# The last expert's down products lag five chunks and close group by group, and the last pair's chain stands in another order

## The chip, the cores and the metric

The kernel runs on one core of one Trainium2 chip. The metric is the device time of one execution in microseconds (us), here the median over several executions. Lower is better.

## What is computed

A block with attention and a mixture of experts, on 16 sequences of 100 tokens with 256 features each:

```python
x = x + attention(layernorm(x), ctx, ctx)      # 16 heads of 16, rope, window of 65 keys
n = layernorm(x).reshape(1600, 256)
topk_p, topk_i = top_k(softmax(n @ router_w.T), 2)
topk_p = topk_p / topk_p.sum(-1)
for e in range(8):                             # gate, up: 1024 x 256; down: 256 x 1024
    mask   = (topk_i == e).any(-1)
    mean_w = (topk_p * (topk_i == e)).sum() / mask.sum()
    x[mask] += mean_w * ((silu(n @ gate[e].T) * (n @ up[e].T)) @ down[e].T)
```

The weight of an expert is one number, the mean over its tokens, so it is known only when the last token has been routed.

## The kernel before

Each engine has a program of its own, written out by hand with semaphores (`s_...`). Engines are named as in the profile: PE (matrix products), DVE and ACT (element-wise work), POOL (small arithmetic and the DMAs that scatter rows), SP (which issues most other DMAs). What an engine's program lists first, it does first; nothing reorders the work.

**Attention.** The 16 sequences are taken in 8 pairs. The loop over `i` and `n` (0 to 7) is a software pipeline: in step `n` of turn `i` an engine does a piece of pair `i`, pieces of pair `i - 1` (output projection, residual), and pieces of pair `i - 2` (normalisation for the router, router, ranks). Scores are made in 64 portions `N`, each of 4 heads of a sequence. `den_transpose` turns the softmax denominators, `attend` (DVE) multiplies them in, `o_project` (PE) projects, `residual` (DVE) adds and takes the statistics, `rows_center` writes the centred rows of the last pair, `x2_transpose` and `route_logits` (PE) lead to `choose` (DVE), which picks two experts. `ranks` counts the tokens of each expert ahead of a token, and POOL's `scatter` writes each row twice into the list of its expert in DRAM (`slots`). `weights_low(-1, 1, k)` splits a sixth `k` of the first expert's weights into a high and a low part (`w_hi`, `w_lo`). `warm` and `idle` are products whose results nobody reads.

**Between the stages.** The first tile of the first expert isn't waited for: `early_tile` transposes what is in the list before the last two pairs, and `late_rows` adds the last two pairs' rows by products with one-hot columns. `here_columns` and `hot_column` make these. `plan` holds how many tiles each expert has.

**Experts.** A tile is 448 rows of one expert, in 4 groups (`GRP`) of 112. In this data each expert has one tile. The 1024 hidden features are 8 chunks (`FC`) of 128. For each chunk `f`, `hidden` makes 12 products for gate and up, ACT applies silu, DVE multiplies, ACT and DVE split the result into `h_hi` and `h_lo`. Experts 0 to 6 make the down products transposed (`columns_down`) and turn them back in the next tile. The last expert makes them in rows (`project_down`), 3 products for each group and chunk: chunk `f - 3` stands behind `hidden(f)`, and the last three chunks follow at the end, first for groups 0 and 1, whose bank is `b_o`, then for groups 2 and 3, whose bank is `b_small`. ACT's `take_output` scales a group into `y_sb`, and POOL adds its 112 rows to the output with an indirect DMA (L1500), four such DMAs in turn.

## Time and profile before

| | us |
|---|---|
| time, median of 3 runs | 466.39 |
| lowest and highest of the 3 | 465.91, 467.24 |
| the profiled execution, its own time | 467.31 |
| its span, first to last instruction | 465.5 |
| PE busy in the span | 443.7 |
| ACT busy | 281.8 |
| DVE busy | 302.2 |
| POOL busy | 138.3 |

Times in the trace count from the start of the span. The profiled execution took 1.81 us more than its span. A matrix product's bar in the timeline is longer than the distance to the next one, since they are pipelined; the distance is what counts in a row of them. For a sequence of like products the timeline gives one row with a count.

### The profile page before, as it was taken

What the parts mean: (1) busy time and instruction counts of PE and PEld (TensorE: products, weight loads), DVE (VectorE), ACT (ScalarE), POOL (GpSimd) and SP (SyncE); (2) the same over time, 40 slices, a digit from 0 to 9 for tenths busy, and PEclk for the clock granted to TensorE, in tenths of its full rate; (3) what the DMA queues carried; (4) which work ended last, traced back from release to release, by engine and by line L of the source; (5) the groups of instructions that cost most, each with busy time, mean ns of one, the idle gap of its engine ahead of it and who ended that gap; (6) DMA issues with size and microseconds to landing.
All of it is one profiled execution on the core that took longest, in us unless ns stands there. A gap on an engine that the chain in (4) does not pass through costs nothing.

```text
span 465.5 us, 8569 instructions
## 1 busy us (share of the span) xinstructions
PE 443.7 (95%) x2553; PEld 358.7 (77%) x2553; DVE 302.2 (65%) x744; ACT 281.8 (61%) x886; POOL 138.3 (30%) x172
## 2 busy tenths in 40 slices
PE   7999999999999999999999999999999999999980
PEld 4657565657566655579999999999999999999980
DVE  3766969798989878787646647467474563763320
ACT  2388778888787888356456456465554655554230
POOL 5201014453626252575014040050220500403122
PEclk9899999999999999899999999999999999999995
DMA  5640092030303032416727636465375453311102
GB/s 166 222 110 8 18 336 73 13 103 18 106 14 112 8 110 68 128 55 199 253 86 180 212 69 180 142 144 172 93 202 174 92 175 85 42 40 21 21 10 30
DMA packets 24667, 49.90 MB, mean 107 GB/s; under 512 B 5730, under 2 KB 15494, under 8 KB 24474
## 3 DMA queue, kind: packets, MB, share of 16 engines
q1 hardware_dynamic: 12858, 22.95, 16.4%
q10 hardware_dynamic: 5616, 19.40, 14.2%
q0 software_dynamic: 6144, 6.97, 8.6%
q8 instruction: 21, 0.34, 0.3%
q14 instruction: 28, 0.23, 0.2%
HBM read 39.16 MB, written 13.20 MB: 112 GB/s over the span
## 4 chain that ended last, share of the span: by engine, by line
PE 80%; DVE 7%; ACT 5%; issue 3%; DMA 1%; POOL 1%; SPq 0%; ACTq 0%; POOLq 0%; DVEq 0%
PE b_s L767 8%; PE b_s L771 8%; PE b_s L768 8%; PE b_small L795 7%; PE b_o L795 7%; PE b_s L490 6%; PE b_pv L513 4%; ACT probs L942 3%; PE b_proj L543 3%; PE b_pt L499 3%; PE b_pt L767 3%; PE b_pt L771 3%; PE b_pt L768 3%; PE b_proj L569 3%; PE b_s L488 3%
## 5 line engine op out<-in xcount | busy, mean ns | idle before, releaser
L942 ACT ACTIVATE probs<-b_s,negmax 100x100 f32<-100x100 f32 x256 | 85.7, 361 | 19.4 <-DVE negmax L1278 19.2
L1500 POOL DMA_INDIRECT out<-y_sb,idnow x32 | 46.8, 1462 | 153.1 <-ACT y_sb L1002 129.8
L975 ACT CAST h_hi<-h_sb 128x448 fp32r<-128x448 f32 x64 | 36.3, 567 | 85.7 <-DVE h_sb L1362 85.7
L1254 DVE TENSOR_TENSOR w_lo<-w_raw,w_hi 128x1024 fp32r<-128x1024 f32 x48 | 58.8, 1224 | 19.5 <-ACT w_hi L906 19.5
L767 PE MATMUL b_s<-x_hi,w_lo 128*128 128x448 f32 x192 | 71.1, 370 | 0.0
L771 PE MATMUL b_s<-x_lo,w_hi 128*128 128x448 f32 x192 | 69.5, 362 | 0.0
L768 PE MATMUL b_s<-x_hi,w_hi 128*128 128x448 f32 x192 | 69.3, 361 | 0.0
L1366 DVE TENSOR_TENSOR h_lo<-h_sb,h_hi 128x448 fp32r<-128x448 f32 x64 | 40.1, 626 | 40.5 <-ACT h_hi L975 40.5
L942 ACT ACTIVATION_READ_ACCUMULATOR probs<-b_s,negmax 100x1 f32 x256 | 56.9, 222 | 0.0
L490 PE MATMUL b_s<-kblk,qrot 128*100 128x400 f32 x128 | 53.6, 499 | 0.0
L906 ACT CAST w_hi<-w_raw 128x1024 fp32r<-128x1024 f32 x48 | 50.4, 1050 | 0.0
L1278 DVE TENSOR_REDUCE negmax<-b_s 100x4 f32<-100x400 f32 x64 | 36.2, 565 | 20.1 <-PE b_s L490 19.8
L1362 DVE TENSOR_TENSOR h_sb<-b_s,act 128x448 f32<-128x448 f32 x32 | 19.8, 620 | 35.2 <-PE b_s L771 35.2
L971 ACT ACTIVATE act<-b_s 128x448 f32<-128x448 f32 x64 | 34.6, 540 | 11.5 <-PE b_s L771 11.3
L1455 POOL DMA_INDIRECT slots<-xrow,desti x32 | 35.3, 1103 | 14.0 <-issue 7.6
L771 PEld LDWEIGHTS b_s<-x_lo,w_hi 128*128 128x128 f32 x192 | 36.0, 188 | 2.7
L767 PEld LDWEIGHTS b_s<-x_hi,w_lo 128*128 128x128 f32 x192 | 36.1, 188 | 2.3 <-ACT x_hi L967 0.3
L499 PEld LDWEIGHTS b_pt<-cst,probs 100*100 100x100 f32 x256 | 26.1, 128 | 15.2 <-issue 14.3
L768 PEld LDWEIGHTS b_s<-x_hi,w_hi 128*128 128x128 f32 x192 | 36.0, 188 | 2.1
L922 ACT COPY probsT<-b_pt 100x400 f32<-100x400 f32 x64 | 32.2, 503 | 4.5 <-PE b_pt L499 4.2
L513 PE MATMUL b_pv<-probsT,v_sb 100*32 100x200 f32 x256 | 31.0, 344 | 3.1 <-ACT probsT L922 2.4
L499 PE MATMUL b_pt<-cst,probs 100*100 100x100 f32 x256 | 32.6, 249 | 0.3 <-ACT probsT L922 0.2
(201 smaller groups left out, 896.7 us busy)
## 6 DMA issues: line engine op xcount, KB each, us to landing
w_raw<-in_ffw ACTq DMA_DIRECT2D x36, 512.0 KB, 4.0
w_raw<-in_ffw SPq DMA_DIRECT2D x12, 512.0 KB, 5.5
slots<-in_padrows SPq DMA_DIRECT2D x9, 449.8 KB, 4.6
xin<-slots SPq DMA_DIRECT2D x9, 449.8 KB, 4.5
kblk<-krot SPq DMA_DIRECT2D x120, 12.5 KB, 1.8
out<-x_all SPq DMA_DIRECT2D x8, 200.0 KB
ctx_all<-in_ctxT SPq DMA_DIRECT2D x1, 1200.0 KB, 6.3
x_all<-in_x SPq DMA_DIRECT2D x1, 1200.0 KB
```

Source lines behind the costliest of these rows:

```text
L490: pe.matmul(o, qrot[:, i % 2, 2 * c + b, :], kblk[:, i % 2, c, h:h + QH, b * S:(b + 1) * S], start=False, stop=True).then_inc(s_s, 1)
L499: m = pe.transpose(b_pt[0:S, h * S:(h + 1) * S], probs[:, N % 3, h, :], ident[0:S, 0:S])
L513: m = pe.matmul(b_pv[32 * j:32 * j + 32, c * PT:(c + 1) * PT], v_sb[:, i % 2, b, c * P + 32 * j:c * P + 32 * j + 32], probsT[:, N % 3, 2 * ...
L767: pe.matmul(o, wl[:, c, cols], x_hi[:, c, :], start=(c == 0), stop=False)
L768: pe.matmul(o, wh[:, c, cols], x_hi[:, c, :], start=False, stop=False)
L771: m = pe.matmul(o, wh[:, c, cols], x_lo[:, c, :], start=False, stop=(c == DC - 1))
L795: m = pe.matmul(b_y[c][:, 0:TILE], left[:, f, c * P:(c + 1) * P], right[:, f, :], start=(f == 0 and k == 0), stop=(f == FC - 1 and k == 2))
L906: nc.scalar.copy(w_hi[1 - par][:, cols], w_raw[:, cols]).then_inc(s_whi, 1)
L942: m = nc.scalar.activation(probs[:, N % 3, h, :], b_s[N % 3][0:S, h * S:(h + 1) * S], ACT.Exp, bias=negmax[:, N % 4, h:h + 1], accum_out=p ...
L1254: V.tensor_tensor(w_lo[1 - par][:, cols], w_raw[:, cols], w_hi[1 - par][:, cols], ALU.subtract).then_inc(s_wlo, 1)
L1366: V.tensor_tensor(h_lo[:, f, :], h_sb[:, f % 2, :], h_hi[:, f, :], ALU.subtract).then_inc(s_hlo, 1)
L1500: G.indirect_dma_start(out, bass.IndirectOffsetOnAxis(idnow[:, n:n + 1], 0), y_sb[:, n, :], None, bounds_check=TOK + TILE - 1, oob_is_err= ...
```

## The change

Five things are done.

1. **The last expert's down products.** Chunk `f - 5` stands behind `hidden(f)` instead of `f - 3`, and the last five chunks follow at the end, group by group: all of group 0, then 1, 2 and 3. Groups 0 and 2 are in `b_o`, 1 and 3 in `b_small`. Each group has a signal of its own.
2. **The last pair's chain.** The residual, the statistics and the centring are done for each of the two sequences apart (`last_residual`), the first while the second is still in attention. `den_transpose` of the last sequence stands before two portions of values. `rows_low(NPAIR - 2)` and, for the last pair's turn, `rows_write` come later. The early tile and the one-hot products are split into pieces between other steps, and the counts of `warm` differ.
3. **The sixth chunk of the first expert's low weights** is made after `meanw`, not during the last pair; PE waits for five chunks at the start of the first expert, and for the sixth before chunk 4 of its down products. SP loads the next weights into that sixth accordingly later.
4. **The start.** SP sends x before the context; the constants go in two pieces, of which the second (4 x 376 bytes a partition of 4 x 1014) goes behind the other weights. The counts of `idle` are 10, 3 and 6 instead of 8, 2 and 3.
5. **The first tile's row numbers** (`idnext`, 448 numbers of 4 bytes) are fetched by a DMA from POOL's queue, behind the scatters, instead of from SP's.

```diff
@@ SP
-            load_rows(0, 0, 1)
-            sp.dma_start(cst[:, :], consts).then_inc(s_cst, 16)
+            sp.dma_start(x_all[:, 0:2, :], x[0:2].rearrange("b s d -> s b d")).then_inc(s_x[0], 16)
+            sp.dma_start(ctx_all[:, :, 0:PT], ctxT[:, :, 0:PT]).then_inc(s_ctx[0], 16)
+            sp.dma_start(cst[:, 0:C_TRI], consts[:, 0:C_TRI]).then_inc(s_cst, 16)
...
-            for k in range(NPAIR - 3, WCH):
-                second_weights(k)
...
+            for k in range(NPAIR - 3, WCH):
+                second_weights(k)
...
-            sp.dma_start(idnext[:, :].bitcast(F32),
@@ PE
                     if n == 5 and i == NPAIR:
-                        warm(5)
-                        early_tile()
-                        warm(5)
+                        warm(8)
                         x2_transpose(NPAIR - 1)
                     if n == 5 and 0 <= i - 2 < NPAIR:
                         ranks(i - 2)
-                    if n == 2 and prv:
+                    if n == 5 and i == NPAIR:
+                        early_tile(0)
+                    if n == 2 and prv and i < NPAIR:
                         den_transpose(2 * i - 1)
...
+                    if n == 1 and i == NPAIR:
+                        den_transpose(2 * i - 1)
...
-            warm(5)
+            late_rows(NPAIR - 2, (1,))
+            warm(2)
             late_rows(NPAIR - 1)
...
-                    o = b_y[g // 2][0:ROWS, g % 2 * D:(g % 2 + 1) * D]
+                    o = b_y[g % 2][0:ROWS, g // 2 * D:(g // 2 + 1) * D]
...
-                    if f == FC - 1 and g % 2:
+                    if f == FC - 1:
                         m.then_inc(s_down, 1)
...
-                    if f >= 3:
-                        (project_down if last else columns_down)(par, t, f - 3)
+                    if f >= 5 and last:
+                        project_down(par, t, f - 5)
+                    elif f >= 3 and not last:
+                        columns_down(e, par, t, f - 3)
...
+                for g in range(GRP):
+                    if g >= DC:
+                        pe.wait_ge(s_y, GRP * t + GRP + g - DC + 1)
+                    for f in range(FC - 5, FC):
+                        project_down(par, t, f, (g,))
                 tile_transpose(t + 1)
...
-                pe.wait_ge(s_wlo, WCH * (e + 1))
+                pe.wait_ge(s_wlo, WCH * (e + 1) if e else WCH - 1)
@@ ACT
                 for n in range(GRP):
-                    if n % 2 == 0:
-                        a.wait_ge(s_down, 2 * t + n // 2 + 1)
+                    a.wait_ge(s_down, GRP * t + n + 1)
@@ DVE
-            def rows_center(i):
...
+            def last_residual(b):
+                i = NPAIR - 1
+                v.wait_ge(s_o, 2 * i + b + 1)
+                v.wait_ge(s_xob, i + 1)
+                xs = x_all[:, 2 * i + b, :]
+                done = s_x2 if b else s_x2a
+                V.tensor_tensor(xs, b_o[0:S, b * D:(b + 1) * D], xs, ALU.add).then_inc(done, 1)
+                v.wait_ge(done, i + 1 if b else 1)
+                link(V.bn_stats(stats2[:, b, :], xs))
+                ins = V.bn_aggr(mv2[:, b, :], stats2[:, b, :])
...
+                V.tensor_scalar(xn[:, b, :], xs, mv2[:, b, 0:1], None, ALU.subtract).then_inc(s_xc, 1)
...
                     if n == 1 and i == NPAIR:
-                        rows_low(NPAIR - 2)
+                        last_residual(0)
...
-                        residual(i - 1)
-                        rows_center(i - 1)
+                        last_residual(1)
...
+                    if n == 3 and i == NPAIR:
+                        rows_low(NPAIR - 2)
...
+            weights_low(-1, 1, WCH - 1)
             for e in range(E - 1):
@@ POOL, behind the last scatter
+            for q in s_scat:
+                g.wait_ge(q, 16 * TOPK * 2 * (NPAIR // 2))
+            g.wait_ge(s_tails[0], 16)
+            G.dma_start(idnext[:, :].bitcast(F32),
```

How the rows of an engine's program stand shows the first two of these best. **PE, end of the last pair's attention**, before: behind the transposes of the last probabilities, from the values (`b_pv`) through the denominators (`rdenx`) and the router's logits (`xn2T`) to the output projection (`att`).

```order
L513 MATMUL b_pv<-probsT,v_sb 32x200 [waits s_pTc]
L513 MATMUL b_pv<-probsT,v_sb 32x200
L513 MATMUL b_pv<-probsT,v_sb 32x200 [waits s_pTc]
L513 MATMUL b_pv<-probsT,v_sb 32x200
L577 MATMUL b_small<-cst,rdenx 128x100 [waits s_x2Tc,s_rx]
L577 MATMUL b_small<-cst,rdenx 128x100
L647 MATMUL b_s<-mask_bf,ident_bf 100x400 x2
L612 MATMUL b_small<-rw_sb,xn2T 100x8 [waits s_rTc,s_x2Tc]
L612 MATMUL b_small<-rw_sb,xn2T 100x8 x3
L647 MATMUL b_s<-mask_bf,ident_bf 100x400
L589 MATMUL b_o<-attw,att 100x256 [waits s_att]
```

The same place in the changed program:

```order
L583 MATMUL b_small<-cst,rdenx 128x100 [waits s_x2Tc,s_rx]
L583 MATMUL b_small<-cst,rdenx 128x100
L519 MATMUL b_pv<-probsT,v_sb 32x200 [waits s_pTc]
L519 MATMUL b_pv<-probsT,v_sb 32x200
L519 MATMUL b_pv<-probsT,v_sb 32x200 [waits s_pTc]
L519 MATMUL b_pv<-probsT,v_sb 32x200
L620 MATMUL b_small<-rw_sb,xn2T 100x8 [waits s_rTc,s_x2Tc]
L620 MATMUL b_small<-rw_sb,xn2T 100x8 x3
L655 MATMUL b_s<-mask_bf,ident_bf 100x400 x4
L597 MATMUL b_o<-attw,att 100x256 [waits s_x2a,s_att]
```

The two transposes of the denominators now stand ahead of the values, and four unread products (`mask_bf`) stand in one piece before the projection.

**DVE, the same stretch**, before: behind the last denominators (`rdenx`), up to the centred rows (`xn`), without the seven rows of `choose` in the middle, which are the same in both programs.

```order
L1126 COPY rdenx<-rden 100x256 [waits s_rT,dve]
L1254 TENSOR_TENSOR w_lo<-w_raw,w_hi 128x1024 [waits s_whi]
L1219 TENSOR_TENSOR xr_lo<-xrow,xr_hi 100x512 [waits s_xrh]
L1133 SCALAR_TENSOR_TENSOR ev<-b_pv,cst,rdenT 128x200 [waits s_rTc,s_pv]
L1135 SCALAR_TENSOR_TENSOR ev<-b_pv,cst,rdenT 128x200
L1140 TENSOR_TENSOR att<-ev 128x200 [waits s_o,dve]
```

```order
L1185 TENSOR_TENSOR sel<-cst,choice 100x32
L1146 TENSOR_TENSOR x_all<-b_o,x_all 100x512 [waits s_xob,s_o,dve]
L1062 BN_STATS stats<-x_all 100x6 [waits s_x2]
L1062 BN_STATS stats<-x_all 100x6
L1066 BN_AGGR mv<-stats 100x2 [waits dve]
L1066 BN_AGGR mv<-stats 100x2
L1154 TENSOR_SCALAR xn<-x_all,mv 100x256 [waits s_var2]
L1154 TENSOR_SCALAR xn<-x_all,mv 100x256
```

And changed:

```order
L1138 COPY rdenx<-rden 100x256 [waits s_rT,dve]
L1169 TENSOR_TENSOR x_all<-b_o,x_all 100x256 [waits s_xob,s_o]
L1171 BN_STATS stats<-x_all 100x6 [waits s_x2a]
L1172 BN_AGGR mv<-stats 100x2 [waits dve]
L1178 TENSOR_SCALAR xn<-x_all,mv 100x256 [waits dve]
L1145 SCALAR_TENSOR_TENSOR ev<-b_pv,cst,rdenT 128x200 [waits s_rTc,s_pv]
L1147 SCALAR_TENSOR_TENSOR ev<-b_pv,cst,rdenT 128x200
L1152 TENSOR_TENSOR att<-ev 128x200 [waits s_o,dve]
```

```order
L1208 TENSOR_TENSOR sel<-cst,choice 100x32
L1169 TENSOR_TENSOR x_all<-b_o,x_all 100x256 [waits s_xob,s_o,dve]
L1171 BN_STATS stats<-x_all 100x6 [waits s_x2]
L1172 BN_AGGR mv<-stats 100x2 [waits dve]
L1178 TENSOR_SCALAR xn<-x_all,mv 100x256 [waits s_var2]
```

The split of weights (`w_lo`) and of rows (`xr_lo`) left this stretch, half of the residual work came ahead of `ev`, and only half of it is left behind `sel`. `xr_lo` now stands behind the four rows of counts and differences that follow `xn`, ahead of the writing of the last pair's rows (`xrow`).

**ACT, the last expert's output**, before:

```order
L988 ACTIVATE y_sb<-b_o,meanw 112x256 [waits s_down]
L988 ACTIVATE y_sb<-b_o,meanw 112x256
L987 REGISTER_ALU
L988 ACTIVATE y_sb<-b_small,meanw 112x256 [waits s_down]
L988 ACTIVATE y_sb<-b_small,meanw 112x256
```

And changed:

```order
L999 ACTIVATE y_sb<-b_o,meanw 112x256 [waits s_down]
L998 REGISTER_ALU
L999 ACTIVATE y_sb<-b_small,meanw 112x256 [waits s_down]
L998 REGISTER_ALU
L999 ACTIVATE y_sb<-b_o,meanw 112x256 [waits s_down]
L998 REGISTER_ALU
L999 ACTIVATE y_sb<-b_small,meanw 112x256 [waits s_down]
```

ACT waited for PE twice, for two groups each; now it waits four times, for one group each.

## Rows read from the trace of the kernel before

**Rows 1.** The page: span, and TensorE's clock in 40 slices, in tenths.

```profile
span 465.5 us, 8569 instructions
...
PEclk9899999999999999899999999999999999999995
```

**Rows 2.** Stretches: us; busy PE, PEld, DVE, ACT, POOL; clock, DMA share, GB/s.

```profile
12.00:13.00 1.00, 1.00 (x5) 1.00 (x4) 0.91 (x3) 0.00 (x0) 0.00 (x0) 0.52 0.93 250
194.00:196.00 2.00, 2.00 (x7) 1.25 (x6) 1.02 (x5) 0.00 (x0) 0.00 (x0) 0.50 0.67 220
250.00:440.00 190.00, 190.00 (x1012) 178.26 (x1011) 108.64 (x154) 102.13 (x170) 37.21 (x31) 1.00 0.47 120
```

**Rows 3.** Timeline of the start: start us, us, engine, line, operation.

```profile
5.90 1.62 PE L543 MATMUL b_proj<-ctx_all,attw 128*128 128x200 f32 x8
7.19 0.75 DVE L1062 BATCH_NORM_STATS2 stats<-x_all 100x6 f32<-100x256 f32 x2 [4.99 <-DMA x_all<-in_x]
...
7.36 1.52 PE L675 MATMUL b_s<-blank 128*128 128x400 bf16 x8
...
10.36 0.53 PE L526 MATMUL b_small<-cst,xn 100*128 100x100 f32 x4 [1.49 <-DVE xn L1078]
...
11.53 2.52 PE L543 MATMUL b_proj<-xnT,attw 128*128 128x200 f32 x8 [0.29 <-issue]
```

**Rows 4.** Timeline from the last pair's attention to the first expert.

```profile
190.11 1.18 PE L513 MATMUL b_pv<-probsT,v_sb 100*32 100x200 f32 x8
...
191.26 0.69 DVE L1219 TENSOR_TENSOR xr_lo<-xrow,xr_hi 100x512 fp32r<-100x512 f32 x1 [0.39 <-ACT xr_hi L901]
...
192.08 0.43 DVE L1133 SCALAR_TENSOR_TENSOR ev<-b_pv,cst,rdenT 128x200 f32<-128x200 f32 x1
...
193.29 2.03 PE L589 MATMUL b_o<-attw,att 128*100 128x256 f32 x4
...
194.32 0.18 DVE L1185 TENSOR_TENSOR sel<-cst,choice 100x32 f32<-100x32 f32 x1
...
195.42 0.69 DVE L1146 TENSOR_TENSOR x_all<-b_o,x_all 100x512 f32<-100x512 f32 x1 [0.92 <-DVE sel L1185]
...
197.21 0.62 DVE L1154 TENSOR_SCALAR xn<-x_all,mv 100x256 f32<-100x256 f32 x2
...
203.65 0.44 PE L666 MATMUL b_proj<-onehot,xr_hi 100*128 100x448 f32 x1
...
206.51 0.47 PE L767 MATMUL b_s<-x_hi,w_lo 128*128 128x448 f32 x1
```

**Rows 5.** Scatters by line (ns min/median/max), then timeline of the second tile's inputs.

```profile
L1455 POOL DMA_INDIRECT slots<-xrow,desti x32: 984/993/1751, 74.7 to 215.1; - x32
...
214.78 1.23 DVE L1254 TENSOR_TENSOR w_lo<-w_raw,w_hi 128x1024 fp32r<-128x1024 f32 x1 [0.30 <-ACT w_hi L906]
...
219.88 0.64 SPq L443 DMA_DIRECT2D idnext<-slots  x1
223.49 0.38 SPq L434 DMA_DIRECT2D xin<-slots  x1
...
229.11 0.56 PE L754 MATMUL b_proj<-cst,xin 112*128 112x112 f32 x4
...
231.10 0.16 DVE L1356 COPY idnext<-xin 112x4 int32<-112x4 int32 x1
```

**Rows 6.** Chain of work at the end; then two rows of the timeline.

```profile
445.86 0.70 PE b_o L782 x6
...
449.36 2.14 PE b_small L782 x18
...
456.15 1.45 POOL out L1500
...
447.15 0.62 DVE L1366 TENSOR_TENSOR h_lo<-h_sb,h_hi 128x448 fp32r<-128x448 f32 x1 [0.63 <-ACT h_hi L975]
...
450.85 1.47 POOL L1500 DMA_INDIRECT out<-y_sb,idnow  x1 [16.03 <-ACT y_sb L988]
```

More of the change, by code:

```diff
@@ L52 @@
 assert MAXTILES < 1 << FIELD
-C_ID, C_TRI, C_ONE, C_MASK = 0, 128, 256, 384
-C_ROPE = C_MASK + S
-C_PAR = C_ROPE + 4 * S
-C_EXP = C_PAR + 2
+C_ID, C_ROPE = 0, 128
+C_MASK = C_ROPE + 4 * S
+C_HEAD = C_MASK + S
+C_PAR = C_HEAD + HC
+C_TRI = C_PAR + 2
+C_ONE = C_TRI + 128
+C_EXP = C_ONE + 128
 C_BASE = C_EXP + E
@@ L593, in x2_transpose @@
             def x2_transpose(i):
-                if i == NPAIR - 1:
-                    pe.wait_ge(s_xc, 1)
-                else:
+                if i < NPAIR - 1:
                     pe.wait_ge(s_xr, i + 1)
@@ L661, in late_rows @@
                 k = i - NPAIR + 2
-                for b in range(2):
+                for b in halves:
                     pe.wait_ge(s_hotA if b else s_hot, k + 1)
@@ L720, in _ @@
                         if i < 0:
-                            idle(8)
+                            idle(10)
                         xn_transpose(i + 1)
@@ L726, in _ @@
                         values(N - 3)
-                    if n == 2 and i == NPAIR:
-                        warm(2)
                     if n == 2 and 0 <= i - 2 < NPAIR:
@@ L807, in output_transpose, with block @@
                         m.then_inc(s_yt, 1)
-            def block(t, par, last, lo):
+            def block(t, e, par, last, lo):
                 for f in range(FC):
@@ L925, in _ @@
                         top_exponentials(i - 2)
-                    if n == 1 and i == NPAIR:
+                    if n == 2 and i == NPAIR:
                         rows_high(NPAIR - 2)
@@ L1149, in residual @@
                 norm_stats(xs, stats2, mv2, s_var2)
-            def rows_center(i):
-                v.wait_ge(s_var2, i + 1)
-                for b in range(2):
-                    ins = V.tensor_scalar(xn[:, b, :], x_all[:, 2 * i + b, :], mv2[:, b, 0:1], None, ALU.subtract)
-                ins.then_inc(s_xc, 1)
+            def last_residual(b):
[8 more added lines that the diff above has]
+                ins = V.bn_aggr(mv2[:, b, :], stats2[:, b, :])
+                if b:
+                    ins.then_inc(s_var2, 1)
+                    v.wait_ge(s_var2, i + 1)
+                else:
+                    link(ins)
+                V.tensor_scalar(xn[:, b, :], xs, mv2[:, b, 0:1], None, ALU.subtract).then_inc(s_xc, 1)
             def rows_write(i):
@@ L1325, in _ @@
                         attend(2 * i)
-                    if n == 6 and prv:
+                    if n == (7 if i == NPAIR - 1 else 6) and prv:
                         rows_write(i - 1)
```

80 lines of the change are left out of this document (43 added, 37 removed).

## The prediction

> **What bounds the kernel now.** I read the page first, then the busy time by stretches, then the chain of work and the timeline at three places. The span is 465.5 us [rows 1]. From 250 to 440 us PE is busy for 190.00 of 190 us at the full clock [rows 2]. The experts, from 206.51 us [rows 4] to the last down product, which ends at 449.36 + 2.14 = 451.50 us [rows 6], are a solid block of products. The change neither adds nor removes a product that counts there, so a gain can only come from the three ends of such blocks: the start, the stretch between attention and the first expert, and what follows the last product. In each the reader should look for what is waited for last.
>
> At the end, POOL's four output DMAs stand one behind the other: the first starts at 450.85, the last at 456.15, and the span ends 465.5 - 456.15 = 9.35 us after that [rows 1, 6]. That remainder (the last DMA's own time, its landing, the closing) I take as fixed.
>
> In the clock row two slices show an 8 [rows 1], the second of them at the last pair. In 12 to 13 us the clock was 0.52 and in 194 to 196 us it was 0.50, that is 1.2 instead of 2.4 GHz, though PE was busy in both [rows 2]. Before the first fall PE stood still from 7.36 + 1.52 = 8.88 to 10.36 us [rows 3].
>
> **The end, term one.** A chunk of down products is 12 products. 18 of them took 2.14 us, 0.117 to 0.119 each, so a chunk is 1.41 us (0.70 + 0.71) and a group's five chunks (15 products) are 1.76 us. Before, hidden(7) was over at 445.86, when chunk 4 began [rows 6]. With a lag of five, two chunks fewer stand ahead of it: it is over at 445.86 - 2.81 = 443.05. Then come chunk 2 (to 444.46) and the groups, to 446.21, 447.97, 449.73 and 451.50. PE ends when it ended before. Before, the first half was closed at 449.36 and POOL's DMA began at 450.85, 1.49 later, with ACT's copy in between [rows 6]; applied to group 0, its DMA begins at 446.21 + 1.49 = 447.70. POOL's own step is (456.15 - 450.85) / 3 = 1.77 us, the same as PE's step of a group, so both rules put the fourth at 452.99 or 453.00 in place of 456.15. **Term: -3.16 us.** A new wait could be group 0's last chunk on `h_lo(7)`. It was there at 447.15 + 0.62 = 447.77, 1.91 us after hidden(7) [rows 6], so it is there by 444.96; PE asks for it after four chunks at 444.46 + 1.41 = 445.87. Group 2 asks for group 0 to be copied out: that is so before POOL starts at 447.70, and it begins at 447.97. Bounds: 0 if POOL found something else to wait for, and at most -3.3, since its four steps can't shrink.
>
> **The start, term two.** x landed at 7.19, second in its queue, and the first context chunk before 5.90, first in it [rows 3]. They are 200 KB each, so I expect them to swap: x near 5.9, the context near 7.2. The key projection, at 5.90 before, then starts 1.3 us later, takes 7.36 - 5.90 = 1.46 us until the next product, and the ten idle products behind it (1.52 us for eight, 1.9 for ten) last until some 10.4. The transposes of xn began at 10.36 [rows 3]. So the earlier x gains nothing by itself; PE is behind it. What is gained is the clock: PE now stands still hardly at all before 11.5, and the query projection, 2.52 us at the low clock against 1.62 for eight like products at the high one [rows 3], is shorter by 0.9. **Term: -0.9 us.** Bounds: +0.1 (the clock falls anyway, and the queue of idle products is a little longer), and -2.2 (the context lands as early as before too, and all of the 1.3 us counts besides). I take the middle, since both ends need something that the rows speak against. Scores, keys and values behind it follow from this projection.
>
> **Between the stages, term three.** By its own clock, before any shift:
> - The attention product `ev` began at 192.08, though the values ended at 190.11 + 1.18 = 191.29; it waited for the denominators, whose transposes stood behind the values [rows 4]. Turned round, it can start at 191.4. I take 191.6, because `rows_write(6)` moved behind the last maximum delays PE's transposes of these rows by an estimated 0.2 us. That is -0.5.
> - `choose` then ends by 194.32 + 0.18 - 0.45 = 194.05. The output projection, 193.29 before, starts at 192.8 and takes 2.03 us at the low clock or about 1.0 at the high one [rows 4]: done at 193.8 or 194.8. The residual, 195.42 before, starts at 194.1 (high clock).
> - From there to the end of centring were 197.21 + 0.62 - 195.42 = 2.41 us for two sequences [rows 4]. For one I take 1.5, more than half since the handovers remain: done at 195.6 in place of 197.83, -2.2. The first sequence's half runs before 191.6, where the split of weights (1.23 us by its kind [rows 5]) and of rows (0.69) stood.
> - That 0.69 [rows 4] returns behind the centring, ahead of the last rows' writing: -1.55 remains, and all of DVE's chain up to the last one-hot columns carries it.
> - PE, between the counts and the last rows' products, has four products of 0.2 and two unread ones instead of five unread ones, and gets to the former 203.65 some 0.2 us later than DVE allows. **Term: -1.35 us**, the first expert at 205.16 instead of 206.51 [rows 4]. Bounds: -0.6 if the clock is low again at the projection (residual at 194.8), and -2.2 if the 0.69 and the 0.2 find room.
>
> **Edits costed at nothing.** The sixth split (1.23 us) now lies ahead of DVE's first work for the expert, which waits for PE's products anyway; PE asks for it six chunks later. It now stands beside POOL's eight scatters. One of these took 1.751 us against a median of 0.993, and it began at 215.1, just behind the start of a split at 214.78 [rows 5]; so I allow them 0.8 us. The Trainium skill, "SBUF — State Buffer", SBUF: two separate sides, says that a VectorE operation with two SBUF inputs and a GpSimd operation that reads SBUF lock each other out for a whole instruction; the slow scatter agrees with this, and by that rule this edit speaks against the change.
> What the scatters delay is the second tile. SP fetched it at 223.49, 3.6 us after it could send `idnext` at 219.88, and PE turned it at 229.11 [rows 5]. Now the scatters start 1.35 to 1.6 us earlier, SP has one DMA less ahead of it (0.64), and PE comes 1.35 earlier: the slack grows by 0.6 to 0.9, which pays the 0.8. If the cover were gone, each us late would be a us of the total.
> `idnext` itself has no row on POOL. Its nearest rows are 0.64 us for the issue on SP [rows 5] and 1.45 us for POOL's 112 rows of output [rows 6], which for 448 elements would be 5.8. From 218.3 with 5.8 and a landing of some 4 it is there by 228; DVE asks for it at 231.10 - 1.35 = 229.75 [rows 5]. Nothing, by either end. The Trainium skill, "DMA: Bandwidth & Descriptors", Issuing engine by pattern, gives simple loads to Sync and calls that path the faster one; by the first-byte figures of its Specifications the move costs 0.4 us, which would be hidden as well.
>
> **Sum.** -3.16 - 0.9 - 1.35 = -5.4 us. The profiled execution, 467.31, becomes 461.9. It stood 0.92 above the median of 466.39, from which the sum gives 461.0. I predict 461.4.
>
> **Rivals.**
> - *The clock falls again in the last pair* (0.2). Its stretch still holds few wide products, and the lengths of its pauses are new. Against it: four unread products in one piece, and more behind. If it falls at the projection, 0.75 is given back; if earlier, over values and logits too, up to 1.7: 462.2 to 463.1.
> - *The start gives nothing* (0.12), because the clock falls there as before: 462.3.
> - *The start gives the whole 1.3 as well* (0.08), as the context is early: 460.1.
> - *The last expert's end gives only half* (0.03): ACT or POOL answer single groups later, or the DMAs land more slowly: 463.0.
> - *The change doesn't do what it says* (0.03): POOL's first DMA starts hardly sooner, and the start gives nothing: 461.4 + 3.2 + 0.9 = 465.5, within 0.3%.
> - *Slower* (0.02). POOL's `idnext` comes so late that DVE stands before the last chunk of the first tile. My upper end leaves 229.75 - 228 = 1.75 us; beyond that each us counts, and from 1.75 + 5.4 = 7.2 us beyond my upper end it decides the sign. At 9 us it gives 461.4 + 7.2 = 468.6.
> The forecast keeps 0.52; its own range is 460.3 to 462.4.
>
> **The numbers.** About 0.3% (1.4 us) is what a measurement of this kernel can tell from no change. All cases but the last two lie beyond it: faster 0.95, same 0.03, slower 0.02. The range takes in the forecast, the clock and both cases of the start: 459.3 to 463.4.
>
> **What would show it.** After: POOL's last four DMAs begin 1.76 apart while PE still multiplies, the first some 3.8 us before PE's last product, the last 1.5 behind it. The clock is 1.00 from 12 to 15 us, the query projection under 1.7 us, while the key projection starts near 7.2. The output projection takes about 1.0 us, the first expert's first product comes near 204.3 in the span (206.51 less 2.25), and PE has no idle time at the second tile. I would be wrong if the clock row kept an 8 at the last pair, if PE waited before group 0's last chunk, or if POOL's DMAs were further apart than before.

## The result, and the profile after

| 13 executions each | before | after |
|---|---|---|
| median, us | 466.32 | 464.93 |
| lowest, highest | 465.91, 467.50 | 460.74, 465.64 |
| profiled execution, us | 467.31 | 465.43 |
| its span, mean clock | 465.5, 0.982 | 463.3, 0.984 |

The ratio of after to before is 0.9939 (95% interval 0.9919 to 0.9960): faster by 1.4 us in the medians, by 2.8 in the means (466.44 and 463.61), whose quotient the ratio is, and by 467.31 - 465.43 = 1.88 in the profiled executions. Predicted were 461.4 and at most 463.4.

The medians hide that the 13 times of after fall apart. The mean granted clock goes with them, but for 462.95: 460.74 and 460.85 at 0.993, 461.29 at 0.995, 461.43 at 0.994; then 462.26 and 462.95 (0.988, 0.984); and seven from 464.93 to 465.64, all at 0.983 or 0.984. The profiled execution is one of the last. Its page shows where the clock went: one slice of 40 at half, which answers to [rows 1].

```profile
span 463.3 us, 8586 instructions
...
PEclk9999999999999999959999999999999999999997
```

The stretches by busy time (us; busy PE, PEld, DVE, ACT, POOL; clock, DMA share, GB/s) answer to [rows 2]:

```profile
12.00:13.00 1.00, 1.00 (x8) 0.64 (x7) 0.62 (x3) 0.50 (x2) 0.00 (x0) 1.00 0.99 314
197.00:199.00 2.00, 1.22 (x7) 0.78 (x8) 1.83 (x13) 0.75 (x2) 1.14 (x4) 1.00 0.00 0
199.00:201.00 2.00, 2.00 (x11) 1.67 (x12) 1.82 (x9) 1.41 (x3) 1.23 (x3) 0.53 0.00 0
201.00:205.00 4.00, 4.00 (x14) 3.56 (x12) 1.47 (x9) 0.88 (x2) 2.75 (x5) 0.50 0.43 117
205.00:209.00 4.00, 4.00 (x14) 3.60 (x14) 3.00 (x11) 1.96 (x4) 3.27 (x3) 0.50 0.63 208
209.00:210.00 1.00, 1.00 (x6) 0.92 (x5) 0.00 (x0) 0.26 (x1) 0.70 (x2) 0.83 0.84 109
250.00:430.00 180.00, 180.00 (x948) 168.67 (x947) 105.22 (x148) 99.16 (x166) 35.76 (x30) 1.00 0.48 126
```

The fall at 12 us is gone. Before the experts the clock is low from 199.1 to 209.3 us, 10.2 us against 3.4 before (193.0 to 196.4), though PE is busy there without a break. My first theory came from the row ahead of it: in 197 to 199 PE was busy for 1.22 of 2 us.

The timeline of the start, beside [rows 3], is the first part below. The second, beside [rows 4], goes from the last pair's attention to the first expert. L597 is the output projection, L1169 the halved residual, L655 `warm`, L635 the ranks, L673 `late_rows`, L776 the experts' first product.

```profile
5.17 0.75 DVE L1073 BATCH_NORM_STATS2 stats<-x_all 100x6 f32<-100x256 f32 x2 [2.95 <-DMA x_all<-in_x]
...
6.62 1.59 PE L549 MATMUL b_proj<-ctx_all,attw 128*128 128x200 f32 x8 [0.94 <-DMA ctx_all<-in_ctxT]
...
9.74 0.51 PE L532 MATMUL b_small<-cst,xn 100*128 100x100 f32 x4
...
10.87 1.59 PE L549 MATMUL b_proj<-xnT,attw 128*128 128x200 f32 x8
...
15.85 0.50 PE L496 MATMUL b_s<-kblk,qrot 128*100 128x400 f32 x1
...
190.07 0.43 DVE L1145 SCALAR_TENSOR_TENSOR ev<-b_pv,cst,rdenT 128x200 f32<-128x200 f32 x1 [0.57 <-PE b_pv L519]
...
191.38 1.03 PE L597 MATMUL b_o<-attw,att 128*100 128x256 f32 x4
...
192.53 0.42 DVE L1169 TENSOR_TENSOR x_all<-b_o,x_all 100x256 f32<-100x256 f32 x1
...
193.60 0.87 PE L610 MATMUL b_small<-cst,xn 100*128 100x100 f32 x4
193.67 0.35 DVE L1178 TENSOR_SCALAR xn<-x_all,mv 100x256 f32<-100x256 f32 x1
...
196.90 0.44 PE L673 MATMUL b_proj<-onehot,xr_hi 100*128 100x448 f32 x1 [0.28 <-DVE onehot L1259]
...
197.78 0.33 PE L655 MATMUL b_s<-mask_bf,ident_bf 100*100 100x400 bf16 x1
...
198.89 0.21 PE L635 MATMUL b_small<-chosen,tri_bf 100*100 100x16 bf16 x1 [0.78 <-DVE chosen L1214]
...
199.13 0.72 PE L673 MATMUL b_proj<-onehot,xr_hi 100*128 100x448 f32 x1
...
201.17 0.84 PE L673 MATMUL b_proj<-onehot,xr_hi 100*128 100x448 f32 x1
...
205.97 0.84 PE L776 MATMUL b_s<-x_hi,w_lo 128*128 128x448 f32 x1
```

From `ev` to the last ranks the chain is earlier, and by more than the start's shift. The scores begin at 15.85 instead of 17.42 (-1.57). `ev` comes at 190.07 instead of 192.08: -2.01, of which -0.44 is its own. The centred rows end at 193.67 + 0.35 = 194.02 instead of 197.21 + 0.62 = 197.83: -3.81, own -2.24. The last pair's one-hot products begin at 201.17 instead of 203.65, and here the clock already eats: the products that follow the first are 0.37 us apart, not 0.20. The first expert begins at 205.97 against 206.51 [rows 4]; of 3.8 us gained 0.5 are left.

At the end (ACT's copy of a group and POOL's DMA, beside [rows 6]):

```profile
447.32 0.47 ACT L999 ACTIVATE y_sb<-b_o,meanw 112x256 f32<-112x256 f32 x1 [1.98 <-PE b_o L791]
...
452.56 0.47 ACT L999 ACTIVATE y_sb<-b_small,meanw 112x256 f32<-112x256 f32 x1 [1.29 <-PE b_small L791]
...
448.70 1.48 POOL L1531 DMA_INDIRECT out<-y_sb,idnow  x1 [12.67 <-ACT y_sb L999]
450.49 1.47 POOL L1531 DMA_INDIRECT out<-y_sb,idnow  x1 [0.30 <-issue]
...
454.03 1.47 POOL L1531 DMA_INDIRECT out<-y_sb,idnow  x1 [0.30 <-issue]
```

POOL's DMAs start 1.77 to 1.79 us apart, and the first goes while PE multiplies for group 1.

### The profile page after: what moved, and what is told of

Its sections match the earlier page's. It is cut to its first block, busy times and chain, and to the rows that moved or that the text cites. A ratio compares the mean times of both kernels' runs of the same rounds, so it can differ in the third digit from the quotient of the medians.

```text
span 463.3 us, 8586 instructions
## 1 busy us (share of the span) xinstructions
PE 444.0 (96%) x2551; PEld 360.9 (78%) x2551; DVE 302.8 (65%) x745; ACT 281.4 (61%) x886; POOL 138.6 (30%) x173
## 4 chain that ended last, share of the span: by engine, by line
PE 54%; POOL 1%; issue 1%; DVE 1%; ACT 0%; POOLq 0%
PE b_s L776 8%; PE b_s L780 8%; PE b_s L777 8%; PE b_small L806 7%; PE b_o L806 7%; PE b_pt L776 3%; PE b_pt L780 3%; PE b_pt L777 3%; POOL out L1531 1%; PE b_o L791 1%; PE b_pv L815 1%; PE b_proj L815 1%; PE b_proj L763 1%; PE b_pv L763 1%; PE b_proj L673 1%
## 5 line engine op out<-in xcount | busy, mean ns | idle before, releaser
L776 PE MATMUL b_s<-x_hi,w_lo 128*128 128x448 f32 x192 | 71.8, 374 | 0.0
L776 PEld LDWEIGHTS b_s<-x_hi,w_lo 128*128 128x128 f32 x192 | 36.6, 190 | 2.2
```

The lines of the kernel that those rows point to most:

```text
L776: pe.matmul(o, wl[:, c, cols], x_hi[:, c, :], start=(c == 0), stop=False)
```

## The experiments

Sixteen kernels ran, in four groups of four, each group on one chip and beside before. Before took 466.44 in the first group, but 472.93, 467.80 and 468.62 in the others, with a wider scatter, so a time is compared within its group. Only the second and the fourth group hold the changed kernel unaltered.

The last column counts executions with a mean clock of 0.988 or less, a line that I chose between the two kinds of the first table. It is a rough sign. The mean takes in every fall, wherever it stands, and the low clock behind PE's last products, 4.7 us in f2_changed_third's profile and 8.0 in f3_fill_again's, 0.005 to 0.009 of the mean; a fall of 3.4 us is worth 0.004. So short falls can hide above the line (a2_end's profile has one, at 0.989). The column is compared only between kernels with the new start.

| kernel | median, us (runs) | ratio to before, 95% | mean clock 0.988 or less |
|---|---|---|---|
| a1_fill | 461.27 (4) | 0.9890, 0.9875 to 0.9904 | 0 of 4 |
| a2_end | 463.56 (5) | 0.9934, 0.9921 to 0.9947 | 0 of 5 |
| a3_start | 465.82 (12) | 0.9986, 0.9978 to 0.9995 | 8 of 12 |
| a4_start_end | 462.78 (5) | 0.9922, 0.9909 to 0.9935 | 0 of 5 |
| b1_changed_again | 463.74 (4) | 0.9804, 0.9745 to 0.9862 | 2 of 4 |
| b2_fill_behind | 466.67 (6) | 0.9873, 0.9825 to 0.9921 | 2 of 6 |
| b3_before_pause | 472.18 (12) | 0.9994, 0.9961 to 1.0027 | 11 of 12 |
| b4_middle_fill | 465.84 (7) | 0.9859, 0.9816 to 0.9903 | 3 of 7 |
| e1_early_late | 463.15 (6) | 0.9886, 0.9835 to 0.9937 | 0 of 6 |
| d1_fill_three | 461.19 (6) | 0.9852, 0.9802 to 0.9901 | 0 of 6 |
| c1_fill_ids_sp | 461.58 (6) | 0.9862, 0.9814 to 0.9910 | 1 of 6 |
| c2_before_again | 470.11 (1) | | 1 of 1 |
| f1_narrow | 463.26 (6) | 0.9861, 0.9812 to 0.9910 | 3 of 6 |
| f2_changed_third | 462.13 (6) | 0.9872, 0.9825 to 0.9919 | 3 of 6 |
| f3_fill_again | 461.13 (6) | 0.9844, 0.9800 to 0.9888 | 1 of 6 |
| f4_wide_ahead | 461.70 (6) | 0.9860, 0.9809 to 0.9911 | 1 of 6 |

**a1_fill: the pause filled.**

```diff
                         late_rows(NPAIR - 2, (0,))
-                        warm(1)
+                        warm(5)
```

> The changed kernel with warm(5) in place of warm(1) behind the first half of the late rows: PE's pause of 0.78 us before the last pair's ranks, after which the granted clock fell to 0.50 at 199.2 us, is filled with four unread products of 0.2 us each. Theory (the clock that fell behind this pause is what is missing): the clock stays 1.00 from 199 to 210 us, the experts' first product comes near 203.2 in place of 205.97, every run lies between 460 and 462 and the median is 460.9. Rival 1 (the fall comes from the whole thin stretch, 184 to 199 us, or from outside the program, and not from this pause): nothing changes, the runs still fall into two groups, near 461 and near 465.4, median above 463. Rival 2 (the four products only delay the ranks and what follows): clock 1.00, but the first expert's product no earlier than 204, 462 or more.

Measured: 461.27, all four between 460.77 and 461.38. By stretches (columns as above), then the experts' first product:

```profile
197.00:199.00 2.00, 1.90 (x16) 1.29 (x15) 1.82 (x14) 0.54 (x1) 0.90 (x4) 1.00 0.00 0
199.00:201.00 2.00, 2.00 (x12) 1.78 (x12) 1.79 (x9) 1.42 (x3) 1.42 (x3) 1.00 0.00 0
201.00:205.00 4.00, 3.99 (x24) 3.34 (x23) 3.49 (x18) 3.00 (x5) 2.69 (x5) 1.00 0.42 117
```

```profile
202.86 0.47 PE L776 MATMUL b_s<-x_hi,w_lo 128*128 128x448 f32 x1
```

The clock is 1.00, and the first product comes 3.11 us earlier than after's 205.97. From the output projection (191.13) to the experts' first product it takes 11.73 us; in after's profile it took 14.59. The unaltered changed kernel was also caught once with the clock at 1.00 throughout (f2_changed_third, last part), and took 203.29 - 191.60 = 11.69. So the four products themselves neither cost nor bring anything; what was missing is the clock. That they kept it up in these four executions does not yet show that they always do, and the pause turns out not to be the cause, as told below.

**a2_end, a3_start, a4_start_end: the parts alone.** These are the kernel before with the hunks of the diff for the last expert's end, for the start (with the `idle` counts), and for both.

> The kernel before with the last expert's end alone (lag of five chunks, groups closed one by one, a signal for each). Theory: this term is 3.2 us wherever the block of experts stands: 466.3 - 3.2 = 463.1, POOL's last DMA 3.2 us sooner than before (near 453.0), PE's last product where it was (451.5), clock before the experts as before. Rival (a part of the end's 3.2 us in the changed kernel came from the later block or from the sixth chunk's place): 464.5 or more, with POOL's four DMAs more than 1.8 us apart or PE waiting for h_lo in the first group.

> The kernel before with the start alone (x first, constants in two pieces, idle products 10, 3 and 6). Theory: x lands near 5.2, the transposes of xn start at 9.7, the query projection takes 1.6 us at the full clock, the first scores come 1.56 us earlier, and nothing behind gives it back: 466.3 - 1.6 = 464.7. Rival 1 (the gain is given back at the last pair, since the pauses or the clock there shift): 465.5 to 466.5, with the clock low for longer than the 3.4 us of before. Rival 2 (the clock at the start and the later clock are one account: what PE does early is taken later): the mean clock of the execution stays at 0.982.

> Start and end together, the last pair and everything between the stages as before. Theory (the terms add up): 466.3 - 1.6 - 3.2 = 461.5, that is 3 us faster than the changed kernel's median, because the clock does not fall for 10 us; all runs within 1 us. Rival (an execution that runs ahead by 1.6 us meets the clock's fall by itself): two groups of runs, or a median above 463.

The end alone gave 466.44 - 463.56 = 2.9 in the medians (by the ratio 3.1, interval 2.5 to 3.7). The start alone gave 0.6, though its profile has the scores at 15.77, the first expert 1.53 earlier than in [rows 4] (204.98) and its own time 1.4 below before's profiled 467.31. Both together gave 3.7, close to 2.9 + 0.6; the theory's 461.5 was missed by 1.3, most of it at the start. From a4_start_end to a1_fill, which adds the rest of the change and the fill, it is 462.78 - 461.27 = 1.5. In a4_start_end the clock was 1.00 at the last pair, and PE stood still all the same:

```profile
191.64 1.11 PE L594 MATMUL b_o<-attw,att 128*100 128x256 f32 x4
...
195.08 0.60 PE L659 MATMUL b_proj<-cst,xin 112*128 112x112 f32 x4 [1.48 <-DMA xin<-slots]
...
196.75 0.42 PE L607 MATMUL b_small<-cst,xn 100*128 100x100 f32 x3
```

The early tile's rows (L659) landed at 195.08. The centred rows, ready at 195.30, were turned (L607) at 196.75, behind the tile and five unread products. In before's first profile the projection at the low clock took that time instead. So the old order lost it in either case, once to the clock and once to a DMA.

**c2_before_again** is before once more, for a second profile.

> The kernel before itself, for a second profile of it. In the first one, 467.31 us, the clock was low twice, 3.4 us each, at the start and in the last pair, with a mean of 0.982; most of its other executions show 0.988 to 0.991 and 466.4. Theory (a typical execution loses only one of the two stretches, and the one at the last pair costs nothing, because PE then waits for the early tile's DMA instead): the mean clock is near 0.99, one of the two stretches is missing, and if it is the one at the last pair, PE shows a wait of about 1.4 us for the early tile's rows. Rival: both stretches are there again, and 467.3 was high for another reason.

Half of it came: one low stretch of 3.4 us in place of two, the mean clock 0.986. But it was the one at the start that was missing: the query projection took 1.59 us, and the scores began at 16.71 where [rows 3]'s execution had them at 17.42. The one at the last pair was there (192.1 to 195.5). The time, 470.11, was high for a reason of another kind, told under the last heading.

**e1_early_late: the early tile moved, nothing else of the last pair's chain.** a4_start_end with `early_tile()` behind `x2_transpose` and `ranks`.

> Start and end as changed, the last pair as before, with one edit in it: the early tile's eight transposes stand behind the transposes of the last pair's centred rows and its ranks (and the five unread products in front of them and the five behind become ten in one piece). In the run with start and end alone PE stood still for 1.48 us until the early tile's DMA was there at 195.08, and turned the centred rows, ready at 195.30, only at 196.75. Theory (what the last pair's new order brings is this wait, more than the halved residual): the centred rows are turned at 195.4, the experts' first product comes near 203.3 instead of 204.62, and the time is 1.3 us below start and end alone: ratio to before 0.9895, where start and end alone had 0.9922. Rival (the chain on DVE decides, the wait was hidden): ratio 0.992, first product at 204.3 or later. If the clock falls in the thin stretch as in the changed kernel: runs 1.5 to 4.5 us above the lowest.

```profile
193.11 1.11 PE L594 MATMUL b_o<-attw,att 128*100 128x256 f32 x4
...
196.82 0.56 PE L607 MATMUL b_small<-cst,xn 100*128 100x100 f32 x4 [0.91 <-DVE xn L1160]
...
197.41 0.58 PE L659 MATMUL b_proj<-cst,xin 112*128 112x112 f32 x4
...
198.72 0.79 PE L617 MATMUL b_small<-rw_sb,xn2T 128*100 128x8 f32 x8
...
205.35 0.47 PE L772 MATMUL b_s<-x_hi,w_lo 128*128 128x448 f32 x1
```

From the projection to the turning it is 3.71 us instead of 5.11, as expected, but from the projection to the experts' first product 12.24 instead of 12.98: 0.74 and not 1.4. The tile's eight transposes, 0.8 us, now stand ahead of the logits (turning to logits 1.90 us). In a1_fill, where only half of them stand there, this distance is 11.73. The first product was expected near 203.3 and came at 205.35, since in this execution the projection itself was 1.47 us later than in a4_start_end (193.11 against 191.64). The median's interval is too wide to add to that.

**b4_middle_fill, c1_fill_ids_sp.** The first is before with the rest of the change and the filled pause, but start and end as before; the second is a1_fill with the row numbers sent from SP.

> The kernel before with the last pair's chain, the sixth chunk and the row numbers' DMA as changed, and with the pause before the ranks filled by four unread products; start and end as before. Theory (terms add up): the changed kernel with the filled pause had 461.3 and start with end alone 462.8, so this part is worth 1.5 us: 466.4 - 1.5 = 464.9. Rival 1 (it is worth more than that alone, 2.5 us or more, and part of it was lost beside the earlier start, where the DMA of the early tile lands last): 464 or less. Rival 2 (worth nothing without the earlier start): 466.

> The changed kernel with the filled pause, and the first tile's row numbers sent from SP's queue as before. Theory (the edit was costed at nothing): the ratio is that of the filled pause, 0.989, within 0.001; SP sends the second tile's rows 0.6 us later, which PE does not notice. Rival 1 (POOL's way is worth something): 0.5 us slower or more, PE waits before the second tile. Rival 2 (POOL's way costs something, since its DMA is issued behind eight scatters): 0.3 us faster or more.

b4_middle_fill had 465.84 where before had 472.93; this says nothing on 1.5 us, since that before was held up otherwise (last heading). Its profile speaks against my theory: the clock fell at 198.4, before the filled place (200.1), and stayed low for 13.7 us with the place filled. c1_fill_ids_sp had 461.58 and 0.9862, between 0.9844 and 0.9890 of the filled pause in two groups: no difference that can be told.

**b3_before_pause, b2_fill_behind: a pause without the thin work, products without the place.**

```diff
 # b3_before_pause, on the kernel before
             m.then_inc(s_cnt, 1)
-            warm(5)
             late_rows(NPAIR - 1)
 # b2_fill_behind, on the changed kernel
             late_rows(NPAIR - 2, (1,))
-            warm(2)
+            warm(6)
```

> The kernel before with the five unread products behind the counts left out (they took 1.03 us from 202.58), so that PE stands still for 1 us before the last pair's one-hot products. Theory (a pause of about this length here is enough to bring the clock down while PE works on): in a part of the executions the clock is 0.50 for 3 to 10 us from about 203, and these take 1.5 to 4.5 us longer than 466.4; the others stay at 466.4; the median lies between 466.4 and 470. Rival (it needs the thin products of the changed order around it, the pause alone does nothing): all runs within 0.5 us of 466.4, clock 1.00 at 203 to 210.

> The changed kernel with the same four extra unread products, but behind the pause: warm(6) in place of warm(2) between the first pair of late rows' second half and the last pair's products; the 0.78 us pause before the ranks stays. Theory (the pause lets the clock fall): the fall at 199.2 stays in most executions, and the four products cost 0.8 to 1.6 us more where they stand: median 465 to 467, with some runs near 462. Rival (what counts is how much PE is given in the whole stretch, wherever it stands): as with the products in the pause, all runs between 461 and 462.5.

b3_before_pause kept before's time (0.9994), and its profile has a pause of 0.93 us with the clock at 1.00 behind it:

```profile
202.00:203.00 1.00, 0.07 (x3) 0.07 (x1) 0.93 (x4) 0.78 (x2) 0.81 (x2) 1.00 0.00 0
203.00:206.00 3.00, 3.00 (x18) 2.75 (x19) 2.58 (x13) 2.00 (x4) 1.90 (x5) 1.00 0.01 3
```

So in this execution a pause of this length did not do it. The rival's own condition, all runs within 0.5 us, was not met (469.87 to 474.18), but before scattered as much. The profile does have a fall, later and elsewhere: at 216.8, inside a pause of 3.55 us in the first expert, of which more under the last heading. b2_fill_behind was 2.9 us slower than the unaltered changed kernel of its group (463.74), and had the low clock in 2 of 6; its scatter (464.67 to 469.98) allows no more than that four products behind did not help. Its profile and that of b1_changed_again show more: the clock fell at 197.1 and at 196.7, at the first late rows, before the place of the 0.78 us pause, which neither execution had, since PE was then slower and DVE no longer behind. In b1_changed_again not every time went with its mean clock: 464.33 and 463.92 had 0.986 and 0.987, 461.66 had 0.994, but 463.57 had 0.993.

**f1 to f4, d1_fill_three: what fills it.** `narrow` is `warm` with 16 columns in place of 400.

```diff
 # f1_narrow, on the changed kernel
                         late_rows(NPAIR - 2, (0,))
                         warm(1)
+                        narrow(16)
 # f4_wide_ahead, on the changed kernel
                     if n == 0 and i == NPAIR + 1:
-                        warm(1)
+                        warm(4)
```

> The changed kernel with the pause before the last ranks filled by 16 narrow unread products (16 columns each, some 0.05 us apart, 0.8 us together) instead of four wide ones (400 columns, 0.2 us apart). PE is then busy in the profile through the pause, but with thin work. Theory A (standing still lets the clock fall): no fall, as with the wide products: all runs near those of the filled pause. Theory B (the thin work does, of which the pause is only the extreme): the falls stay, times in two groups and a median as in the unaltered changed kernel on this chip, 2 us or more above the filled pause.

> The changed kernel with three more wide unread products ahead of the last logits (near 194.8), and the 0.78 us pause left open. They stand on the chain of the last pair, so they cost up to 0.6 us where the clock is the same. Theory A (the pause): falls as in the unaltered kernel, median 463 or more. Theory B (how much wide work there is in the thin stretch, wherever it stands): falls rarer than in the unaltered kernel, median near 461.9.

> The changed kernel, unaltered, on the chip of these runs. Both theories: runs between 461 and 466 with the clock low for 3 to 14 us in most of them, median 1.5 us or more above the filled pause.

> The filled pause (four wide unread products) again, on the chip of these runs. If it cures the fall on this chip too: median near 461.3 and mean clock 0.991 or more in at least four of five runs. If the falls depend on where in the stretch the execution stands when it comes there: a part of the runs at 0.988 or less, 1.5 to 4.5 us longer.

> The changed kernel with unread products at three places: one more ahead of the last logits, one ahead of the first half of the late rows (where PE stood still for 0.28 us), four more in the 0.78 us pause. The clock fell at 196.6 to 198.5 us in three executions on another chip, before the pause is reached, so filling the pause alone can't cure it there. Theory (the thin stretch from 193.4 on, and not the pause alone, lets the clock fall): all runs within 1 us, mean clock 0.991 or more in each, median 0.2 us above the filled pause alone; ratio 0.989 to 0.990. Rival (the fall is chance in the stretch, whatever is put in): some runs 1.5 to 4.5 us above the lowest, with a mean clock under 0.988.

With narrow products three of six had the low clock (465.13, 465.28, 466.63), like the unaltered kernel's three of six. With wide ones, in the pause or ahead of it with the pause left open, it was one of six each. The counts lean to theory B, but three of six against one of six, or against two of twelve, can be chance, and the unaltered kernel's median, 462.13, was only 1.0 above the filled pause's 461.13, where 1.5 or more was expected. d1_fill_three had none of six at 0.988 or less, but one of 463.73 at 0.989, and so not all runs within 1 us. In f1_narrow's profile the clock was low for 13.7 us. It fell at 196.7, again before the place of the pause, and PE had no pause in it beyond 0.29 us:

```profile
196.00:197.00 1.00, 0.71 (x5) 0.53 (x5) 1.00 (x3) 0.97 (x2) 0.92 (x2) 0.84 0.00 0
...
199.00:201.00 2.00, 2.00 (x22) 1.96 (x22) 0.51 (x3) 0.53 (x2) 1.36 (x4) 0.50 0.00 0
...
205.00:210.00 5.00, 5.00 (x18) 4.55 (x17) 3.52 (x11) 2.58 (x5) 4.09 (x4) 0.50 0.80 251
```

Over all groups: the unaltered changed kernel had the mean clock at 0.988 or less in 14 of 23 executions (9 of 13, 2 of 4, 3 of 6); with wide unread products in or ahead of the pause it was 3 of 28, or 6 of 35 with b4_middle_fill, which fills the pause behind the old start. That is far apart, but most of it compares groups on different chips. Theory A cannot account for the four profiles in which the clock fell before the pause was reached (b1, b2, b4, f1); that the wide products make the long falls rarer is likely and not shown.

## Why the prediction failed

**The end (-3.16) was right.** Alone it measured 2.9 in the medians (by the ratio 2.5 to 3.7). Within the profile the experts' block runs 1.07 us late (the first turning of outputs at 210.10 against 209.03) and the last DMA starts at 454.03, 2.12 before the former 456.15 [rows 6]: 3.19. PE did not wait for `h_lo(7)`, and the remainder behind the last DMA is 463.3 - 454.03 = 9.27 us against 9.35.

**The start (-0.9) was about right in size, for a wrong reason.** x came at 5.17 and not near 5.9, the context at 6.62 and not at 7.2, so PE was some 0.6 earlier than I had it; with the query projection 1.59 us long instead of 2.52 the scores came 1.57 us sooner. (The prediction's own sum for the idle products is 7.2 + 1.46 + 1.9 = 10.56, not 10.4, which changes nothing in it.) I had taken the fall at 12 us for a property of the kernel. It is one of some executions: the scores began at 17.42 and 18.05 in two profiles of the old start that have it, and at 16.71, 16.77 and 17.41 in three that have not, against 15.26 to 16.55 in the thirteen of the new start, with a median of 15.65. Against an execution without the fall the scores are 1.1 to 1.8 us sooner by that median, and the median of a3_start says that 0.6 arrive at the end.

**Between the stages (-1.35) the terms held where the clock stayed up, with one cause that I had not seen.** `ev` -0.44 (forecast -0.5), centred rows -2.24 (forecast -2.2), the whole 1.5 from a4_start_end to a1_fill. But I explained the old order's delay by the clock at the projection and by DVE's chain. The early tile's DMA stood right behind, ready to take the same 1.4 us when the clock was high; moving half of the tile behind the logits is part of what the change brings.

**Edits costed at nothing** show no cost in the trace; only the row numbers' DMA was tried apart (c1_fill_ids_sp). `idnext` left POOL at 215.72 and POOL had copied it on at 221.97, the second tile's transposes had no wait, one scatter took 1.446 us (it began at 207.71, 0.63 us behind the moved split), and nobody waited for it. By the lock that the Trainium skill describes ("SBUF — State Buffer", SBUF: two separate sides) this was to be expected, and the trace agrees.

**The step that failed is the rival "the clock falls again in the last pair"**: a chance of 0.2, and a price of 0.75 to 1.7 us. The mean clock was at 0.988 or less in 9 of the 13 executions of the result. The seven slowest take 465.35 in the mean, the four fastest 461.08: 4.3 us. The one of the seven with a profile has the fall of 10.2 us, and beside f2_changed_third's profile of the same program without a fall its experts begin 205.97 - 203.29 = 2.7 us later and its last output DMA 454.03 - 449.94 = 4.1 us later. For the chance I counted "four unread products in one piece, and more behind". What the listing of the order shows, and I did not add up, is the place behind them: from the turning of the centred rows at 193.6 to the late rows at 196.9 there is one wide unread product, where before had 3 and 3 (198.2 to 200.5); and behind the first late rows there is one and a pause, where before had the second four of them. Whether that is why the falls are longer or more frequent no run settles. For the price I took the one length that before's trace shows, 3.4 us, and places no later than the projection, and so the range ended at 463.4. In after's profile the fall came 7.7 us behind the projection's start, lasted 10.2 us and ran into the experts' own products. Where the clock stays up the sum itself is met: 460.74 to 461.43 in the result, and 461.13 to 461.58 as medians of the three kernels with only the pause filled (one of them with the row numbers from SP), where the sum had given 461.0 and 461.9.

My first theory after the result (the pause lets the clock fall) fell too: in b1_changed_again, b2_fill_behind, b4_middle_fill and f1_narrow the clock fell before the place of the pause, and in b3_before_pause the clock stayed at 1.00 for 13.8 us behind a pause of 0.93 us. What is shown is that the same program takes some 4 us more when the clock falls here for 10 us. That wide unread products in this stretch make such falls rarer is what the counts suggest. What exactly starts one is not settled.

## What to carry to other kernels

Before an edit takes unread products out of a stretch of small products and waits, count what is left there in the new order, stretch by stretch, and price a fall of the clock at several lengths, not at the one that a trace happens to show. When times of one kernel lie in two groups, read the clock of each execution before reading the median, and then a trace of each kind, since the mean does not say where the clock was low. Four products of 0.2 us put where PE would stand anyway went with 461.3 instead of 464.9 in one pair of groups, and with 461.1 instead of 462.1 within another, where it is inside the noise. And when a wait is removed, ask what was landing just behind it: here a DMA was ready to take its place.

## What was unexpected in the hardware

**The low clock lasts for very different lengths under a busy PE.** 3.4 us (before, twice; a2_end, a3_start, c2_before_again), 6.8 (b1_changed_again, from 196.7; b2_fill_behind, twice; b3_before_pause), 10.2 (after) and 13.7 (b4_middle_fill, f1_narrow), PE at 100% in nearly all of it, but for the second fall of b2_fill_behind and that of b3_before_pause, which began while it stood still. In after it came back while the experts' products ran, not during the late rows and the small products of the weights' sum. Why it took so long in one execution and 3.4 us in another stays open.

**The same program does and does not fall.** f2_changed_third's profile has the same order, the same pause of 0.78 us and the clock at 1.00 throughout:

```profile
199.12 0.21 PE L635 MATMUL b_small<-chosen,tri_bf 100*100 100x16 bf16 x1 [0.78 <-DVE chosen L1214]
...
203.29 0.47 PE L776 MATMUL b_s<-x_hi,w_lo 128*128 128x448 f32 x1
```

```profile
199.00:201.00 2.00, 1.88 (x15) 1.69 (x16) 1.85 (x9) 1.42 (x3) 1.09 (x2) 1.00 0.03 8
201.00:205.00 4.00, 4.00 (x24) 3.38 (x22) 3.42 (x20) 2.65 (x5) 2.86 (x6) 1.00 0.38 110
```

The Trainium skill, "TensorE: Matmul & The Clock Gate", What's actually happening, says that the activity watch runs free of the program, so that the point of change varies. The trace agrees in part: counted from the start of the output projection, the falls of the last pair in like programs began 7.7 us behind it in after, but 5.5, 5.5, 5.5 and 5.9 us in b1_changed_again, b4_middle_fill, f1_narrow and b2_fill_behind. The same section gives an idle spell as what brings the clock down. Two falls fit that: they began inside pauses of 3.55 us (b3_before_pause) and 3.15 us (b2_fill_behind). A pause of 3.28 us in c2_before_again brought none, nor did one of 1.48 in a4_start_end or one of 1.91 at the start of b4_middle_fill, and in the falls of the last pair of the changed order the longest pause behind the projection was 0.78 us.

**In the later groups before was held up in its first expert.** In c2_before_again ACT stood still for 4.26 us behind the split of weights, ahead of an `act`, with "remote" named as its releaser, and PE lost 3.28 us:

```profile
210.78 1.05 ACT L906 CAST w_hi<-w_raw 128x1024 fp32r<-128x1024 f32 x1
216.09 0.54 ACT L971 ACTIVATE act<-b_s 128x448 f32<-128x448 f32 x1 [4.26 <-remote]
...
217.53 0.47 PE L767 MATMUL b_s<-x_hi,w_lo 128*128 128x448 f32 x1 [3.28 <-DVE h_sb L1362]
```

b3_before_pause shows the same (3.55 us of PE), and b2_fill_behind 3.15; the profiled executions of the other versions had 0 to 1.6. In those two the clock fell while PE stood still and stayed low for 6.8 us. In b3_before_pause, by stretches:

```profile
213.00:214.00 1.00, 0.88 (x5) 0.48 (x3) 0.00 (x0) 0.12 (x1) 0.69 (x2) 1.00 0.25 54
...
216.00:217.00 1.00, 0.00 (x0) 0.00 (x0) 0.25 (x1) 0.00 (x0) 0.00 (x0) 0.89 0.36 103
217.00:218.00 1.00, 0.57 (x2) 0.53 (x3) 0.38 (x1) 0.59 (x2) 0.00 (x0) 0.50 0.00 0
```

From the experts' first product to the last output DMA it took 461.83 - 205.52 = 256.31 us, where [rows 6]'s execution took 456.15 - 206.51 = 249.64: 6.67 more, of which the pause is 3.55 and the rest about half of the 6.8 us at the low clock. So in these groups a low mean clock need not mean a fall in the last pair. A pause of 3.3 us, alone or with such a fall behind it (6.7), is of the size by which before was slower in the later groups (1.4 to 6.5 us), and the ratios there are lower than in the first. No run looked for its cause, and it is left open; the terms above are taken from the first group and from within traces.
